# Two key tiles to a TensorE visit in the first attention, and a prologue in another order

## What is computed

```python
def _attn(q, k, v):
    s = jnp.einsum('bhqd,bhkd->bhqk', q, k) * SCALE
    p = jax.nn.softmax(s, axis=-1)
    return jnp.einsum('bhqk,bhkd->bhqd', p, v)
...
q = _ln((x @ Wq + bq).reshape(b, s1, H, HD), qn_w, qn_b)
kv = jnp.concatenate([y_main @ Wk + bk, y_main @ Wv + bv], axis=-1)
kv = kv.reshape(b, s2, H, 2 * HD)
k = _ln(kv[..., :HD], kn_w, kn_b)
v = kv[..., HD:]
...
ctx = ctx + DCA_WEIGHT * ctx_dca
return ctx @ Wo + bo
```

## Time and profile before

| | us |
| --- | --- |
| median of 3 runs | 2095.7 (2092.73 to 2102.14) |
| the profiled execution | 2102.49 |
| its span, first to last instruction | 2100.8 |
| first scores of the first attention | 67.97 |
| step 5 of batches 0, 1, 2, 3 | 81.65, 182.24, 282.04, 381.94 |
| end of the attention's windows | 445.50 |
| TensorE busy over the span | 1934.4 (92%) |
| ScalarE busy over the span | 1047.8 (50%) |
| VectorE busy over the span | 1157.4 (55%) |

### The profile page before, as it was taken

How to read it: one execution, slowest core, us unless ns; L and a number is a source line. 1 busy time by engine, 2 the same in 40 slices (tenths; PEclk the granted TensorE clock), 3 DMA queues, 4 the chain that set the end, 5 groups by cost and what they waited for, 6 DMA issues and landing times.

```text
span 2100.8 us, 29802 instructions
## 1 busy us (share of the span) xinstructions
PE 1934.4 (92%) x9157; PEld 1262.5 (60%) x9159; DVE 1157.4 (55%) x1916; ACT 1047.8 (50%) x1697; POOL 293.1 (14%) x276
## 2 busy tenths in 40 slices
PE   5789898977999799999999999999999995999998
PEld 2333333336888575665666666666666664788886
DVE  6544545334666574455745467444664455466665
ACT  1466666742333365556655556555665552232232
POOL 2000000004444110000000000000000002345452
PEclk9799999987999899999999999999999996899999
DMA  2302111107544110000100001000000001244443
GB/s 72 82 22 61 40 43 34 34 9 222 117 108 115 32 32 0 0 0 0 32 0 0 0 0 32 0 0 0 0 1 0 0 0 35 60 111 114 114 109 78
DMA packets 107055, 89.79 MB, mean 43 GB/s; under 512 B 71812, under 2 KB 93448, under 8 KB 106344
## 3 DMA queue, kind: packets, MB, share of 16 engines
q1 hardware_dynamic: 106984, 88.85, 16.8%
HBM read 73.73 MB, written 1.44 MB: 36 GB/s over the span
## 4 chain that ended last, share of the span: by engine, by line
PE 84%; DVE 9%; ACT 2%; issue 2%; POOL 2%; DMA 1%; ACTq 0%; SPq 0%; DVEq 0%; POOLq 0%
PE ps L1096 17%; PE ps L1033 16%; PE ps L387 15%; PE ps L398 8%; PE ps L905 6%; PE ps L918 6%; PE ps L1110 3%; PE ps L1044 3%; PE ps L850 2%; DVE s_rk L1554 2%; POOL s_stage L678 1%; PE ps L1068 1%; PE ps L1105 1%; DVE s_rq L1550 1%; PE ps L1061 1%
## 5 line engine op out<-in xcount | busy, mean ns | idle before, releaser
L817 ACT ACTIVATE s_p<-ps,s_g,s_rk 128x256 f32<-128x256 f32 (+1 forms) x832 | 417.5, 561 | 300.4 <-PE ps L1033 270.4
L1033 PE MATMUL ps<-s_qq,s_ctxT 128*128 (+2 forms) x1248 | 500.7, 514 | 2.7 <-ACT s_ksq L791 2.7
L1096 PE MATMUL ps<-s_p,s_ctx 128*128 128x512 f32 (+1 forms) x832 | 418.3, 597 | 12.8 <-ACT s_p L817 12.8
L1586 DVE TENSOR_TENSOR s_dsum<-s_dsum,s_p 128x512 f32<-128x512 f32 (+1 forms) x384 | 265.9, 692 | 236.6 <-ACT s_p L817 225.0
L387 PE MATMUL ps<-s_xT,s_wgus 128*128 128x512 f32 x1440 | 350.7, 393 | 2.6 <-DVE s_hw L1482 2.6
L1033 PEld LDWEIGHTS ps<-s_qq,s_ctxT 128*128 128x128 f32 (+1 forms) x1248 | 232.0, 186 | 201.2 <-issue 163.7
L387 PEld LDWEIGHTS ps<-s_xT,s_wgus 128*128 128x128 f32 x1440 | 273.0, 190 | 61.4 <-DVE s_hw L1482 3.0
L733 ACT ACTIVATE s_p<-ps,s_bsm 128x1024 f32<-128x1024 f32 x208 | 231.1, 1114 | 113.4 <-PE ps L905 107.1
L1096 PEld LDWEIGHTS ps<-s_p,s_ctx 128*128 128x128 f32 (+1 forms) x832 | 157.7, 190 | 76.9 <-ACT s_p L817 24.6
L1484 DVE TENSOR_TENSOR s_hs<-s_hw,s_hs 128x512 fp32r<-128x512 f32 x120 | 140.5, 1171 | 82.5 <-ACT s_hs L338 82.5
L398 PE MATMUL ps<-s_hs,s_wds 128*128 128x512 f32 x720 | 183.2, 390 | 1.8 <-DVE s_hs L1484 1.8
(11 more groups left out here) (230 smaller groups left out, 1726.2 us busy)
## 6 DMA issues: line engine op xcount, KB each, us to landing
s_wB<-w1s SPq DMA_DIRECT2D x64, 256.0 KB, 3.9
s_kT<-s_kst SPq DMA_DIRECT2D x64, 128.0 KB, 2.3
s_wB<-w0s SPq DMA_DIRECT2D x16, 384.0 KB, 3.6
s_kT<-s_kst SPq DMA_DIRECT2D x64, 80.0 KB, 2.1
s_wB<-w0s SPq DMA_DIRECT2D x16, 256.0 KB, 4.0
s_wgu<-in_L_ffn_Wg_dram SPq DMA_DIRECT2D x64, 64.0 KB, 2.6
s_wgu<-in_L_ffn_Wu_dram SPq DMA_DIRECT2D x64, 64.0 KB, 2.4
s_wd<-in_L_ffn_Wd_dram SPq DMA_DIRECT2D x64, 64.0 KB, 2.4
```

The costliest lines, as they stand in the source:

```text
L817: ins = nc.scalar.activation(p1[0:r, BANK1[t], j, :], ps[0:r, BANK1[t], j * SQ:(j + 1) * SQ], ACT.Exp, bias=g1[0:r, 3:4], scale=rk_col(t, ...
L1033: ins = nc.tensor.matmul(out, lhs(x_), rhs(y_), start=first and n == 0, stop=last and n == 2)
L1096: nc.tensor.matmul(ps[:, 4, :], ctx1[0:ROWS1[t], t, :], p1[0:ROWS1[t], BANK1[t], :, :].rearrange("p a n -> p (a n)"), start=t == 0, stop=t ...
L1586: v.tensor_tensor(dsum[0:r, :], dsum[0:r, :], pt[0:r, :], ALU.add).then_inc(s.summed, 1)
```

## The change

TensorE now goes through the steps in pairs (a visit): the side work of the first step, the scores of the steps n+3 and n+4, the side work of the second step, the values of both. There are three score slots (banks 0 to 5) and four slots for probabilities; what was two side banks is one (`MISCBANK`, 7), and what was two sum banks is one (`SUMBANK`, 6). A score tile takes two matmuls of 128 rows: `kT0` holds each head pair's rows as rounded, rest, rounded, rest (four blocks of 32), and `qz` has the rounded queries on rows 0 to 63 and the rest on rows 64 to 127. `kT0` holds one batch, and is filled by 32 DMAs for each half of the heads instead of 16. Queries are copied four times before their transposes, of which there are four a group instead of two. Squares have two buffers. VectorE copies a group's sums (`keep_sums`) apart from working on them (`read_sums`), and its order is changed; so are the tables of TensorE's side work. In the prologue the key weights are centred first and the projections go ahead of all query products; ScalarE evicts the first turned keys; `bounds` comes after the first queries.

```diff
-TURN1 = (0, 1, 3, 4)
-PROJ = (5, 7, 9, 10, 12, 14, 15, 17, 19, 21, 23, 24, 26)
-TURN0 = (37, 39, 41, 42)
-QUERY = (8, 20, 33, 46)
-SUMS = (16, 28, 43)
-SQUARE = (27, 28, 29, 30, 31)
-ROOT = 33
+TURN1 = (0, 1, 2, 3)
+PROJ = (5, 6, 8, 9, 11, 12, 14, 16, 18, 19, 21, 22, 24)
+TURN0 = (35, 37, 38, 40)
+QUERY = (7, 20, 32, 44)
+SUMS = (17, 33, 41)
+SQUARE = (25, 26, 27, 28, 29)
+ROOT = 31
...
+        MISCBANK, SUMBANK = 7, 6
...
-                    for j in range(4):
-                        g, r = 2 * half + j // 2, 64 * (j % 2)
-                        for lo in range(2):
-                            sp.dma_start(kT0[r + 32 * lo:r + 32 * lo + 32, b % 2, g, cols].bitcast(F32),
-                                         kst[32 * j:32 * j + 32, lo, cols].bitcast(F32)).then_inc(landed(half, part), 16)
+                    for g in (2 * half, 2 * half + 1):
+                        if b and part == 0:
+                            sp.wait_ge(s.scores0, primed(STEPS0 * (b - 1) + KT * (g + 1)))
+                        for i in range(2):
+                            r = 64 * (g % 2) + 32 * i
+                            for k in range(4):
+                                sp.dma_start(kT0[32 * k:32 * k + 32, g, i, cols].bitcast(F32),
+                                             kst[r:r + 32, k % 2, cols].bitcast(F32)).then_inc(landed(g, part), 16)
...
-                pe.wait_ge(s.misc_read, primed(m - 1))
+                pe.wait_ge(s.misc_read, primed(m))
...
-                pe.wait_ge(s.probs0, primed(n - 1))
+                pe.wait_ge(s.probs0, primed(n - 2))
...
-                for part in range(2):
-                    for i in range(2):
-                        rows = slice(64 * i, 64 * i + 64)
-                        ins = nc.tensor.matmul(ps[:, 2 * (n % 2) + i, :], kT0[rows, b % 2, g, t * P:(t + 1) * P],
-                                               qz[rows, g % 2, part, :], start=part == 0, stop=part == 1)
+                for i in range(2):
+                    ins = nc.tensor.matmul(ps[:, 2 * (n % 3) + i, :], kT0[:, g, i, t * P:(t + 1) * P], qz[:, g % 2, i, :],
+                                           start=True, stop=True)
...
-                    pe.wait_ge(s.o0_read, primed(b * NG + g - 1))
+                    pe.wait_ge(s.o0_read, primed(b * NG + g))
...
-            pe_turn(pe, 0)
+            pe_turn_start(pe, 0)
             pe.wait_ge(s.w0_centered, 1)
-            for t in range(TB):
-                project_queries(t)
             for t in range(KT):
                 project(0, t)
-            for t in range(TB, NT):
+            pe_turn_end(pe, 0)
+            pe.wait_ge(s.wq_centered, 1)
+            for t in range(NT):
                 project_queries(t)
...
+            for n in range(3):
+                scores_at(n)
             for b in range(B):
+                for step in range(0, STEPS0, 2):
+                    n = b * STEPS0 + step
+                    prepare(b, step)
+                    scores_at(n + 3)
+                    scores_at(n + 4)
+                    prepare(b, step + 1)
                     values(b, step)
+                    values(b, step + 1)
                 turn_sums(b, NG - 1)
...
-                for k in range(TB):
-                    pair = k * H0 // 2 + 2 * g
-                    ins = nc.tensor.transpose(ps[:, bank0(m), k * P:(k + 1) * P],
-                                              qd[:, pair:pair + 2].rearrange("p n r h d -> p (n r h d)"), ident[:])
+                for i in range(2):
+                    for k in range(TB):
+                        ins = nc.tensor.transpose(ps[:, MISCBANK, i * SQ + k * P:i * SQ + (k + 1) * P],
+                                                  qd[:, k * H0 // 2 + 2 * g + i].rearrange("p r d -> p (r d)"), ident[:])
...
-                me.do(v.tensor_copy(qz[:, g % 2, 0, :], f))
-                v.tensor_tensor(qz[:, g % 2, 1, :], f, qz[:, g % 2, 0, :].bitcast(F32), ALU.subtract).then_inc(s.qz_ready, 1)
+                q = qz[:, g % 2]
+                me.do(v.tensor_copy(q, kf[:]))
+                v.tensor_tensor(q[64:P], kf[64:P], q[64:P].bitcast(F32), ALU.subtract).then_inc(s.qz_ready, 1)
...
-                read_sums(b, 1)
+                keep_sums(b, 1)
                 if more:
-                    query_variance(b + 1)
                     key_variance(b + 1)
                 read_queries(b, 3)
+                read_sums(b, 1)
                 if more:
                     inverse_std(b + 1)
                     scale_keys(b + 1, 0)
                     scale_keys(b + 1, 1)
                     scale_queries(b + 1)
-                    for c in range(4):
+                    for c in range(3):
                         read_keys(b + 1, 0, c)
+                keep_sums(b, 2)
+                if more:
+                    read_keys(b + 1, 0, 3)
                 read_sums(b, 2)
```

More of the change, by code:

```diff
@@ L410, in pe_turn_back, with squares, landed @@
                 ins.then_inc(s.y_turned, 1)
-        def bank0(m):
-            return 6 + m % 2
-        def landed(half, part):
-            return ((s.kT_landed00, s.kT_landed01), (s.kT_landed10, s.kT_landed11))[half][part]
+        MISCBANK, SUMBANK = 7, 6
+        def squares(b, g):
+            n = KT * HG * D0 if g < NG else TB * D
+            if b == 0:
+                return p0[:, 2 + g % 2, 0:n]
+            return xnT[:].rearrange("p k n -> p (k n)")[:, (b + g) % 2 * NT * P:(b + g) % 2 * NT * P + n]
+        def landed(g, part):
+            return ((s.kT_landed00, s.kT_landed01), (s.kT_landed10, s.kT_landed11),
+                    (s.kT_landed20, s.kT_landed21), (s.kT_landed30, s.kT_landed31))[g][part]
         def group_of(ap, g):
@@ L723, in _ @@
             nc.scalar.activation(bsm[:, 6:12], bsm[:, 0:6], ACT.Sqrt).then_inc(s.bound_root, 1)
+            for c in range(4):
+                m = MISC["keys", 0, 0, c]
+                act.wait_ge(s.misc_made, m + 1)
+                n, part = (HALF, 1) if c < 3 else (P, 2)
+                for j in range(part):
+                    cols = slice(j * n // part, (j + 1) * n // part)
+                    ins = nc.scalar.activation(p0[:, c, cols], ps[:, MISCBANK, cols], ACT.Identity,
+                                               bias=wcol[:, 3 + 2 * j:4 + 2 * j], scale=wcol[:, 2 + 2 * j:3 + 2 * j])
+                ins.then_inc(s.kf_made, 1)
             act.wait_ge(s.bound0_ready, 1)
@@ L1243, in _, with center @@
             starts = np.cumsum([0] + [n for _, n in centered])
-            for (w, n), c in zip(centered, starts):
-                me.did(v.tensor_reduce(s1[:, c:c + n], w, AX, ALU.add))
-            me.wait()
-            me.do(v.tensor_scalar(s1[:, 0:starts[-1]], s1[:, 0:starts[-1]], 1.0 / D0, None, ALU.mult))
-            for j, ((w, n), c) in enumerate(zip(centered, starts)):
-                ins = v.tensor_tensor(w, w, bc(s1[:, c:c + n], D0), ALU.subtract)
-                if j < len(centered) - 1:
-                    me.did(ins)
-                else:
-                    ins.then_inc(s.w0_centered, 1)
-            take_turned(0)
+            def center(js, done):
+                for j in js:
+                    me.did(v.tensor_reduce(s1[:, starts[j]:starts[j + 1]], centered[j][0], AX, ALU.add))
+                me.wait()
+                cols = slice(starts[js[0]], starts[js[-1] + 1])
+                me.do(v.tensor_scalar(s1[:, cols], s1[:, cols], 1.0 / D0, None, ALU.mult))
+                for j in js:
+                    ins = v.tensor_tensor(centered[j][0], centered[j][0], bc(s1[:, starts[j]:starts[j + 1]], D0), ALU.subtract)
+                    if j < js[-1]:
+                        me.did(ins)
+                ins.then_inc(done, 1)
+            center((0, 1, 2), s.w0_centered)
             def bounds():
@@ L1289, in _ @@
             KQ = KT * H0
[L1291 to L1294 removed]
             def key_variance(b):
[L1298 to L1302 removed]
+                for g in range(NG + 1):
+                    dve.wait_ge(s.k_squared, 5 * b + g + 1)
+                    to = s2[:, g * KT * HG:(g + 1) * KT * HG] if g < NG else s2[:, KQ:]
+                    v.tensor_reduce(to, squares(b, g).rearrange("p (m d) -> p m d", d=D0), AX, ALU.add).then_inc(s.k_sq_read, 1)
+                dve.wait_ge(s.k_sq_read, primed(5 * (b + 1)))
                 v.tensor_scalar(s2[:], s2[:], 1.0 / D0, 1e-6, ALU.mult, ALU.add).then_inc(s.k_var, 1)
@@ L1394, in _ @@
             scale_queries(0)
-            bounds()
             for c in range(4):
@@ L1398, in _ @@
             read_queries(0, 0)
+            bounds()
             scale_keys(0, 2)
@@ L1430, in _ @@
                     scale_keys(b + 1, 3)
+                keep_sums(b, 3)
                 read_sums(b, 3)
```

172 lines of the change are left out of this document (89 added, 83 removed).

## The result

| | before | after |
| --- | --- | --- |
| median, us | 2097.95 (11 runs) | 2107.56 (11 runs, 2103.1 to 2111.76) |
| span of the profiled execution | 2100.8 | 2106.2 |
| first scores | 67.97 | 80.12 |
| projection of step 5, batch 0 | 81.65 | 100.67 |
| last turn of sums | 445.55 | 448.79 |

After over before is 1.0042, with a 95% interval of 1.0026 to 1.0057: 0.4% slower, inside the 0.5% that was called no change, and 2.6 us from the predicted 2105. In us it lies just above 2106, the bound that the prediction drew from the earlier median of before (2095.7), where it had put a chance of 0.33.

The account below looks back on a forecast made before the run. TensorE sets the pace, with ScalarE close behind. Profiled 2102.5 us + 23.4 (prologue, clock) - 9.0 (three batches) - 5.3 (last stretch) = 2111.6; less 6.8 for the median, 2104.8, given as 2105, range 2084 to 2120.

Parts of the forecast that it names:

- Visit: TensorE's pair of steps: 2.10 us, bounds 2.00 to 2.20; fewer changeovers save time, full height saves no streaming.
- Batches: First attention's three batches, cut at step 5: 97.1 us each against 100.1, saving 3.0 each.
- X: Steps 26 to 39: ScalarE's last exponential before the root, 8.4 us after step 25; step 39 ends at X+21.3.
- Queries at steps 7 and 20: The projection behind the query turn waits 0.6 us for the bank, the next 0.8 for VectorE: 2.8 a batch.
- Sum copies: At steps 13 and 39 TensorE stands still 0.85 us for the copy of the sums and two handovers.
- Last stretch: The last 47 steps, without preparation: 58.3 us against 63.6, saving 5.3.
- Prologue: One-bank projections at half clock, reads ending at 57.3; first scores 83.3 (+15.3 us), step 5 at 104.0 (+22.4).
- The copies: Key copies, 32 SyncE issues a half, not 16: all land 22.9 us after the first, not hidden in batch 0.
- The full clock in the projections: Rival for the first projections: rounds of 1.98 us, reads end at 46.7, 12 us less, 2093; chance 0.22.
- The side bank's round trip: Rival: it exceeds its 2.06 us reuse, 39 projections in the steps wait some 0.5 each: 20 us, 2125; chance 0.13.
- set the pace of the visits: Rival: ScalarE binds, steps at 1.10 instead of 1.05, 9 us, 2114; chance included in the forecast's 0.50.
- the waits overlap: Rival: 5.5 us a batch of added waits may fall into ScalarE's stalls; batches 91.6, whole taken as 2082; chance 0.15.

Follow-up runs that it names:

- single tiles: Changed kernel with full-height scores, three slots and one side bank, but one key tile a visit: 2117.89 us, 1.0104 of before.
- the old key rows: Changed kernel with the key rows and queries of the kernel before (16 copies a half, half-height matmuls, two transposes a query turn): 2091.66 us, 0.9964 of before.
- two banks: Changed kernel, but the first batch's odd projections go to bank 6, the even ones stay in bank 7: 2087.25 us, 0.9944 of before.
- split copies: Changed kernel, but batch 0's first-half 32 key copies are issued half by SyncE, half by ScalarE: 2103.15 us, 1.0021 of before.
- the last kernel: The combination plus second-tile scores between the value products at group ends and an early one-element exponential on ScalarE: 2062.02 us, 0.9822 of before.
- the filled loop: Changed kernel with one bank, plus an unread 448-column product into bank 5 behind each of the 13 first projections: 2097.61 us, 0.9989 of before.
- the combination: Changed kernel with two banks for first projections, old key rows and queries, keys scaled before group 1's sums are read, early bounds: 2062.93 us, 0.9811 of before.

## Why the prediction was right, step by step

The time came out by sums of the right mechanisms with errors on both sides. That it is only 2.6 us off is in part luck: at the end of the attention the sum was 5.9 us too high, and a loss behind it that nobody forecast and the reference point of the median made that up.

- **Visit.** 2.10 forecast, 2.14 measured; full height saves no streaming, shown twice (a step of 1.23 with either height, a visit of 2.13 with either). The prediction put the saving in the changes of kind, and a step without side work is 0.16 shorter; in the whole kernel single tiles cost only 10.3 us.
- **Batches.** 97.1 forecast; 98.3, 95.5 and 95.6 measured, 289.4 in place of 291.3. (The 1.0 that the sum adds for a clock still at half is in the first: the projection at 100.67 took 1.94 where the next took 1.12.) The stretch from the sum copy behind step 25 to the end of step 39's values took 30.5 (143.47 to 174.01) for 29.7 forecast. X was the end of the exponential at 152.11, the first key turn came at X + 12.0 as worked out. VectorE's order in it, named as the cause, was worth 4.3 us in the trace and 8.8 in the time.
- **Queries at steps 7 and 20.** After's chain that ended last shows the round trip, as start, duration, what: TensorE goes from the query turn through VectorE's four instructions and the reads to the next projection.

```profile
106.37 0.81 DVE s_kf L1403
107.18 0.73 DVE s_kf L1404
...
107.94 0.70 DVE s_qz L1407
...
108.66 1.22 DVE s_qz L1408
...
109.92 0.42 DVE s_kx L1259
110.34 0.34 DVE s_vg L1257
...
110.73 1.13 PE ps L873 x2
```

The two waits were 0.72 and 0.73, forecast 0.6 and 0.8. The estimate of 1.22 for the subtraction on 64 partitions is what it took. But shortening this chain in the run with the old key rows gave little, 1.3 us over the first batch and nothing in the second; that a wait at one place was made up at another is likely, but was not followed up.
- **Sum copies.** 0.85 forecast, 0.91 where both products have work in one visit, 1.18 at step 39.
- **Last stretch.** 58.3 forecast, 58.7 measured.
- **Prologue.** The step that was off. First scores 83.3 forecast, 80.12 measured, and step 5 104.0 against 100.67. The half clock was right for ten of the rounds, with the idle 0.8 in each (0.85), but it was taken from the first one, and the first three were at the full clock: 3 x 0.86 = 2.6 too much, less 0.08 too little for most of the others. The last reads ended at 55.0 for the 57.3 forecast. This is the term that was mis-sized. Behind it the queries' projections took 7.61 instead of 10.0, and the chain to the second key tile 17.9 (54.98 to 72.85) instead of 18.6. The copies were sized right: 21.24 us for 32 issues and the last landing near 95.6, 22.7 after the first issue, forecast 22.9; VectorE stood 5.95 us for it. The first scores waited for the queries (79.86) and not for the landing of their eight copies; but this came at about the same time, near 79.95, if the copy issued until 77.90 took 2.05 to land as the last one did (an estimate).
- **Behind the attention.** Nothing was forecast here, and about 2 us lie here. The 16 transposes before the output projection took 3.60 us in after and 1.97 in before; the granted clock over them was 0.54 and 1.00. It is no property of the visits: two banks, split copies and the last kernel have these 1.6 us too, the other runs do not; the output projection starts 4.9 us later where the last turn of sums was 3.2 later.

TensorE's timeline of after:

```profile
448.79 0.66 PE L914 MATMUL ps<-s_ident,s_oT 128*128 128x128 f32 x4 [0.82 <-DVE s_oT L1413]
450.58 3.60 PE L997 MATMUL ps<-s_ident,s_xn 128*128 128x128 f32 x16 [1.14 <-DVE s_xn L1423]
456.33 8.86 PE L1002 MATMUL ps<-s_wo,s_xnT 128*128 128x256 f32 x32 [2.14 <-ACT s_xnT L770]
```

and the same of before:

```profile
447.34 1.97 PE L964 MATMUL ps<-s_ident,s_xn 128*128 128x128 f32 x16 [1.13 <-DVE s_xn L1377]
451.45 8.86 PE L969 MATMUL ps<-s_wo,s_xnT 128*128 128x256 f32 x32 [2.14 <-ACT s_xnT L747]
```

- **By sum.** Forecast +23.4 - 9.0 - 5.3 = +9.1 on the profiled execution. Measured +19.0 - 10.9 - 4.9 = +3.2 at the end of the attention, and +5.4 in the span. The medians differ by 9.6, since before's profiled execution lay 4.5 above the median of before and after's (2107.87) 0.3 above its own. The forecast took 6.8 off for this, by the three runs then shown, and so an error of 3.7 too much on the profiled execution became 2.8 too little on the median. The difference of the medians, 9.6, is close to the forecast 9.1, but through other terms.
- **Rivals.** The full clock in the projections did not happen in after, but it is what the filled loop shows (2097.61; the rival said 2093, with the reads ending at 46.7, where its own rounds of 1.98 give 46.1 and the filled loop 45.6). The side bank's round trip did not bind the steps: in batch 0 of after the projections at 113.82, 123.26, 126.89 and 128.86 begin with no idle time ahead, and those at 107.96, 110.73, 133.30 and 136.07, behind query turns, with 0.65 to 0.80. ScalarE did not set the pace of the visits: its exponentials follow at 1.06 us in the last batch (six in 6.39), which is TensorE's pace. But TensorE did wait for exponentials, once in the last batch (1.16 at 413.45) and in the three batches 14 times, 14.2 us in all; in before these are 16.2 us in 9 waits. That the waits overlap was true to 1.9 us only.

What the change lost is shown by the runs: one bank in the prologue (20 us), doubled key rows (16), sums read before the keys are scaled (9 by the medians, 4 in the trace). What is left with the losses taken away shows in the combination's 1.9%, some 36 us under before by the medians and 40 by the ratio. By place, its profiled execution has step 5 at 71.78, 9.9 us earlier than before (the new prologue and the first five steps), and takes 334.5 us from there to the last turn of sums for 363.9, 29.4 less. These 29.4 hold the pairing, but also the double buffer of the squares and VectorE's new order; they were not told apart.

## What to carry to other kernels

A pairing of like work on TensorE pays by fewer changes of kind, here 0.16 us in a step without side work and some 10 us in the whole, and it does not need the matmuls to be of full height where two row tiles run side by side already. Count what the pairing takes away elsewhere: every bank that it needs is missing in the prologue too, where nothing hides the round trip, and there a bank that is still unused can be borrowed. A loop of matmuls with a gap in each round may cost twice, by the gap and by the clock; look at the granted clock of the stretch before a wait is priced.

## What was not expected of the hardware

- In the one-bank loop the granted clock falls at another place from one execution of the same projections to the next: in after at 23.8, in the run with split copies and in that with one tile at 19.8, in that with the old key rows only at 28.0. Each round is 0.95 us longer from there, and the start of the last projection lies between 48.39 and 51.95, so this alone moves what follows by up to 3.6 us. TensorE's timeline with the old key rows:

```profile
26.05 1.12 PE L871 MATMUL ps<-s_wkv,s_ctxT 128*128 128x512 f32 x2 [0.85 <-DVE s_vg L1257]
28.03 1.98 PE L871 MATMUL ps<-s_wkv,s_ctxT 128*128 128x512 f32 x2 [0.85 <-DVE s_vg L1257]
30.85 2.07 PE L871 MATMUL ps<-s_wkv,s_ctxT 128*128 128x512 f32 x2 [0.85 <-DVE s_vg L1257]
```

- Two queues of issues do not halve their time: 0.88 us each on ScalarE and 0.81 on SyncE, where SyncE alone takes 0.66; the 32 issues took 15.3 us together (74.86 to 90.11) in place of 21.2.
- The table load of ScalarE does not run ahead of the wait of the instruction that needs it (it starts 1.26 to 1.30 us after the first scores and takes 1.28, three kernels); an exponential of one element ahead of the wait brings it forward.
